# A transformer block with kernelized attention and routed experts on one core: the fifth weighing of the values moved to VectorE, the second norm's scalings put between copies, shorter GpSimd chains, a direct last store

## What is computed

```python
mod = (silu(c) @ wmod)                 # six vectors of 256 per batch row: sa, ca, ga, sb, cb, gb
h = layernorm(x) * (1 + ca) + sa       # x: 8 x 1024 x 256
x = x + ga * attention(h)
h = layernorm(x) * (1 + cb) + sb
x = x + gb * ffn(h)

# attention, 16 heads of 16: q, k, v from one product; xq, xk = clip(q / 4), clip(k / 4)
Tq, Tk = chebyshev(xq), chebyshev(xk)            # polynomials of the orders 0 to 10, 5 of which have a weight
num = sum over orders of Tq * beta * cumsum over tokens of (Tk * v)
den = sum over orders of sum(Tq) * beta * cumsum over tokens of sum(Tk)
attention = (num / (den + 1e-7)) @ W_out.T

# ffn: one shared expert and the best 2 of 8 routed ones, weights sqrt(softplus(logits)), hidden size 128
```

## Time and profile before

| | us |
|---|---|
| median of three timed runs | 977.48 |
| lowest and highest of them | 973.81, 977.93 |
| the profiled execution | 972.85 |
| its span, first to last instruction | 971.1 |
| TensorE busy | 861.6 (89%) |
| VectorE busy | 836.6 (86%) |
| GpSimd busy | 474.3 (49%) |
| ScalarE busy | 441.0 (45%) |

### The profile page before, as it was taken

How to read it: one execution, slowest core, us unless ns; L and a number is a source line. 1 busy time by engine, 2 the same in 40 slices (tenths; PEclk the granted TensorE clock), 3 DMA queues, 4 the chain that set the end, 5 groups by cost and what they waited for, 6 DMA issues and landing times. The chain is left out here.

```text
span 971.1 us, 14288 instructions
## 1 busy us (share of the span) xinstructions
PE 861.6 (89%) x4377; PEld 642.1 (66%) x4377; DVE 836.6 (86%) x1317; ACT 441.0 (45%) x636; POOL 474.3 (49%) x636
## 2 busy tenths in 40 slices
PE   5765839899999989899999999898999999979995
PEld 4535436686767676776767676766767676747784
DVE  2797879999999999999999999999999999987421
ACT  4624345554636354555535363555545363521420
POOL 2525354554637265645737274645746274443210
PEclk9786769999999999999999999999999999989998
DMA  8023125353534445364535344453534343444331
GB/s 303 1 50 88 23 67 163 67 153 74 152 81 100 126 77 159 66 155 85 163 66 141 76 91 139 82 158 67 163 69 128 76 116 98 80 124 83 121 109 22
DMA packets 52237, 101.03 MB, mean 104 GB/s; under 512 B 5380, under 2 KB 34639, under 8 KB 50135
## 3 DMA queue, kind: packets, MB, share of 16 engines
q1 hardware_dynamic: 36340, 66.14, 20.9%
q0 software_dynamic: 15360, 33.56, 20.2%
q10 hardware_dynamic: 482, 0.74, 0.2%
HBM read 57.68 MB, written 17.58 MB: 77 GB/s over the span
## 5 line engine op out<-in xcount | busy, mean ns | idle before, releaser
L1425 PE MATMUL acc<-w,hid 128*128 128x256 f32 x1152 | 272.9, 382 | 13.2 <-DVE hid L1116 13.2
L1425 PEld LDWEIGHTS acc<-w,hid 128*128 128x128 f32 x1152 | 215.7, 190 | 57.1 <-DVE hid L1116 24.1
L795 ACT ACTIVATE hid<-ring,b1row 128x512 f32<-128x512 f32 x144 | 98.5, 684 | 180.3 <-PE ring L1306 179.0
L618 POOL DMA_DIRECT2D feat<-feat x48 | 46.5, 968 | 269.4 <-DVE feat L993 132.4
L1116 DVE TENSOR_TENSOR hid<-hid,cfw 128x512 f32<-128x512 f32 x128 | 92.4, 724 | 39.0 <-DMA cfw<-cf_rows 23.6
L750 ACT ACTIVATE feat<-ring,bqkv 128x512 f32<-128x512 f32 x96 | 66.1, 689 | 112.4 <-PE ring L1306 112.4
L1306 PE MATMUL ring<-n2H,w1H 128*128 128x512 f32 x288 | 102.3, 436 | 0.0
L1383 PE MATMUL tr<-wo_g,feat 128*128 128x256 f32 x256 | 64.7, 410 | 40.0 <-DVE feat L1035 40.0
L968 DVE TENSOR_TENSOR_SCAN feat<-zero,carry,feat 128x512 f32<-128x512 f32 x80 | 99.3, 1291 | 0.0
L968 DVE TENSOR_TENSOR_SCAN feat<-zero,feat 128x512 f32<-128x512 f32 x80 | 95.8, 1247 | 0.0
L1306 PE MATMUL ring<-n2H,w1L 128*128 128x512 f32 x288 | 90.8, 396 | 0.0
(11 more groups left out here) (160 smaller groups left out, 1571.4 us busy)
## 6 DMA issues: line engine op xcount, KB each, us to landing
feat<-feat POOLq DMA_DIRECT2D x48, 512.0 KB, 4.6
cfw<-cf_rows SPq DMA_DIRECT2D x16, 1280.0 KB, 7.6
xin<-in_L_attn_x SPq DMA_DIRECT2D x16, 512.0 KB, 9.3
feat<-inv_rows SPq DMA_DIRECT2D x32, 256.0 KB
out<-x SPq DMA_DIRECT2D x16, 512.0 KB, 8.5
cfw<-cf_rows SPq DMA_DIRECT2D x16, 512.0 KB, 3.7
out<-fin POOLq DMA_DIRECT2D x16, 512.0 KB, 6.0
cfw<-cf_rows SPq DMA_DIRECT2D x16, 256.0 KB, 4.6
```

Source lines behind the costliest of these rows:

```text
L618: g.dma_start(f(into), f(of), accum_op=ALU.add).then_inc(added[n], 16)
L795: a.activation(hid[:, e % NG], ring[bank][:, :], ACT.Silu, bias=b1row[:, e:e + 1]).then_inc(ring_copied, 1)
L1425: last = mm(acc[t // 2][:, t % 2], hid[:, e % NG, t * P:(t + 1) * P], w2[:, e], start=False, stop=(e == E), skip_group_check=True)
```

## The change

Five edits.

1. The weighing of order 4 (`KT5 * V0`) leaves GpSimd (`weigh_order_5` and its semaphore go) and becomes the fourth of five weighings on VectorE, after expert 3 and ahead of the weighing of order 2 (order `BY_WEIGHT`). The waits on the counts follow.
2. `normalise_second` is called four times, one scaling behind each of the four k and q copies. The first call has the two waits, the last one raises the semaphore.
3. `inv_std` (both norms) has ten operations for twelve: the halving of the mean is folded into the variance's constants, and the inverse deviation is doubled at the end.
4. For the last chunk alone: no store of x1, and no accumulating store. `last_output` on VectorE gates each bank, adds x1, and SyncE stores each half of the output directly. SyncE's last waits follow.
5. For the last chunk alone: TensorE holds back the `expert_down` of experts 6 and 7 and does those of 6, 7 and 8 for bank 0 first, then for bank 1 (`last_experts_by_bank`).

```diff
@@ inv_std
-            nc.gpsimd.tensor_tensor(t(0), m0, m1, ALU.add).then_inc(mv_steps[n], 1)
             nc.gpsimd.tensor_tensor(t(1), m0, m1, ALU.subtract).then_inc(mv_steps[n], 1)
             nc.gpsimd.tensor_tensor(t(2), s0, s1, ALU.add).then_inc(mv_steps[n], 1)
-            pool.wait_ge(mv_steps[n], NMV * c + 3)
-            nc.gpsimd.tensor_tensor(t(3), t(0), k_("half", NT), ALU.mult).then_inc(mv_steps[n], 1)
-            nc.gpsimd.tensor_tensor(t(4), t(1), k_("half", NT), ALU.mult).then_inc(mv_steps[n], 1)
-            nc.gpsimd.tensor_tensor(t(5), t(2), k_("1/D", NT), ALU.mult).then_inc(mv_steps[n], 1)
+            nc.gpsimd.tensor_tensor(t(0), m0, m1, ALU.add).then_inc(mv_steps[n], 1)
+            pool.wait_ge(mv_steps[n], NMV * c + 2)
+            nc.gpsimd.tensor_tensor(t(6), t(1), t(1), ALU.mult).then_inc(mv_steps[n], 1)
+            nc.gpsimd.tensor_scalar(t(7), t(2), 4.0 / D, 4.0 * EPS_LN, ALU.mult, ALU.add).then_inc(mv_steps[n], 1)
+            pool.wait_ge(mv_steps[n], NMV * c + 5)
+            nc.gpsimd.tensor_tensor(t(8), t(6), t(7), ALU.add).then_inc(mv_steps[n], 1)
+            nc.gpsimd.tensor_scalar(t(10), t(0), -1.0, None, ALU.mult).then_inc(mv_steps[n], 1)
             pool.wait_ge(mv_steps[n], NMV * c + 6)
-            nc.gpsimd.tensor_tensor(t(6), t(4), t(4), ALU.mult).then_inc(mv_steps[n], 1)
-            nc.gpsimd.tensor_tensor(t(7), t(5), k_("eps", NT), ALU.add).then_inc(mv_steps[n], 1)
+            nc.gpsimd.tensor_tensor(t(3), t(8), k_("-half", NT), ALU.pow).then_inc(mv_steps[n], 1)
             pool.wait_ge(mv_steps[n], NMV * c + 8)
-            nc.gpsimd.tensor_tensor(t(8), t(6), t(7), ALU.add).then_inc(mv_steps[n], 1)
-            pool.wait_ge(mv_steps[n], NMV * c + 9)
-            nc.gpsimd.tensor_tensor(t(9), t(8), k_("-half", NT), ALU.pow) \
-                .then_inc(mv_steps[n], 1)
-            nc.gpsimd.tensor_tensor(t(10), t(0), k_("-half", NT), ALU.mult).then_inc(mv_steps[n], 1)
-            pool.wait_ge(mv_steps[n], NMV * c + 11)
-            nc.gpsimd.tensor_tensor(t(11), t(10), t(9), ALU.mult).then_inc(rstd_ready[n], 1)
+            nc.gpsimd.tensor_tensor(t(9), t(3), t(3), ALU.add).then_inc(mv_steps[n], 1)
+            nc.gpsimd.tensor_tensor(t(11), t(10), t(3), ALU.mult).then_inc(rstd_ready[n], 1)
@@ SyncE
-                if loads or i < B:
+                if i < B and not is_last(i, p):
                     store_x1(i, p)
...
+            for h in range(2):
+                sp.wait_ge(out_added, h + 1)
+                sp.dma_start(o_v[B - 1, CB - 1][:, 2 * h:2 * h + 2], fin[:, 2 * h:2 * h + 2]).then_inc(last_stored, 16)
...
+            sp.wait_ge(last_stored, 2 * 16)
@@ GpSimd
-                g.tensor_tensor(f(W + 4), f(KT5), f(V0), ALU.mult).then_inc(weighted5, 1)
...
-                    weigh_order_5(i, p)
...
-                if st["ffn"]:
+                if st["ffn"] and not is_last(*later(i, p, -2)):
                     add_to_output(*later(i, p, -2))
@@ ScalarE
-                for half in HALVES[:4]:
+                for t, half in enumerate(HALVES[:4]):
                     copy(half)
-                if second:
-                    normalise_second(act, *prev)
+                    if second:
+                        normalise_second(act, *prev, t)
@@ VectorE
-            BY_WEIGHT = (0, 1, 3, 2)
+            BY_WEIGHT = (0, 1, 3, 4, 2)
...
+                    dve.wait_ge(odd_ready, 4 * c + n // 2)
+                    v.tensor_tensor(f(W + n), f(KT3 if n == 2 else KT5), val, ALU.mult).then_inc(weighted, 1)
...
+            def last_output(i, p):
+
+                dve.wait_ge(gate_loaded[1], 16 * (i + 1))
+                dve.wait_ge(stored[1 - p], 16 * (i + p))
+                for h in range(2):
+                    rows = fin[:, 2 * h:2 * h + 2]
+                    dve.wait_ge(bank_done, h + 1)
+                    v.tensor_tensor(rows, acc[h][:, :, :], gate(1), ALU.mult).then_inc(ffn_gated, 1)
+                    dve.wait_ge(ffn_gated, 2 * number(i, p) + h + 1)
+                    v.tensor_tensor(rows, rows, x1[:, p, 2 * h:2 * h + 2], ALU.add).then_inc(out_added, 1)
...
                 expert(3)
                 if attn_:
                     weigh(i, p, 3)
+                    weigh(i, p, 4)
                     prefix(i, p, 2)
                     prefix(i, p, 3)
@@ TensorE
+            def last_experts_by_bank(i, p):
+
+                c = number(i, p)
+                for h in range(2):
+                    for e in (E - 2, E - 1, E):
+                        if h == 0:
+                            pe.wait_ge(hidw_ready, E * c + e)
+                        for t in (2 * h, 2 * h + 1):
+                            last = mm(acc[h][:, t % 2], hid[:, e % NG, t * P:(t + 1) * P], w2[:, e], start=False,
+                                      stop=(e == E), skip_group_check=True)
+                    last.then_inc(bank_done, 1)
```

More of the change, by code:

```diff
@@ L234, in build @@
         weighted = sem("values_weighted")
-        weighted5 = sem("values_weighted_order_5")
         scanned = sem("prefix_sums")
@@ L257, in build @@
         hidw_ready = sem("hidden_weighted")
-        expert_done = sem("expert_done")
+        expert_done, bank_done = sem("expert_done"), sem("bank_done")
+        out_added, last_stored = sem("output_added"), sem("last_stored")
         ffn_gated = sem("ffn_gated")
-        NLOG, NSOFT, NCF, NSPLIT, NMV = 7, 10, 3, 7, 11
+        NLOG, NSOFT, NCF, NSPLIT, NMV = 7, 10, 3, 7, 9
         late_products, late_biases, late_weights = (sem(f"late_{n}") for n in ("bias_products", "biases", "weights"))
@@ L286, in number, with is_last @@
             return CB * i + p
+        def is_last(i, p):
+            return isinstance(i, int) and number(i, p) == CB * B - 1
         def later(i, p, n):
@@ L386, in normalise_first, with normalise_second @@
             last.then_inc(norm_ready[0], 1)
-        def normalise_second(act, i, p):
+        def normalise_second(act, i, p, t):
             c = number(i, p)
[L391 to L396, removed]
+            if t == 0:
+                act.wait_ge(rstd_ready[1], c + 1)
+                ge(act, transposed[1], 2 * c)
+            last = nc.scalar.activation(ntok[:, t], x1[:, p, t], ACT.Identity, bias=ms[:, 1, 11, t:t + 1],
+                                        scale=ms[:, 1, 9, t:t + 1])
+            if t == NT - 1:
+                last.then_inc(norm_ready[1], 1)
         def load(sp, i, p):
@@ L591, in _ @@
                     step(i, p, True, False)
-            for p in range(CB):
-                sp.wait_ge(x1_stored[p], 16 * B)
-                sp.wait_ge(stored[p], 16 * B)
+            for h in range(2):
+                sp.wait_ge(out_added, h + 1)
+                sp.dma_start(o_v[B - 1, CB - 1][:, 2 * h:2 * h + 2], fin[:, 2 * h:2 * h + 2]).then_inc(last_stored, 16)
+            sp.wait_ge(x1_stored[0], 16 * B)
+            sp.wait_ge(stored[0], 16 * B)
+            sp.wait_ge(x1_stored[CB - 1], 16 * (B - 1))
+            sp.wait_ge(stored[CB - 1], 16 * (B - 1))
+            sp.wait_ge(last_stored, 2 * 16)
         @block.gpsimd
@@ L599, in _ @@
             g = nc.gpsimd
-            def weigh_order_5(i, p):
-                c = number(i, p)
-                pool.wait_ge(odd_ready, 4 * c + 2)
-                ge(pool, numerator, c)
-                g.tensor_tensor(f(W + 4), f(KT5), f(V0), ALU.mult).then_inc(weighted5, 1)
             def add_orders(i, p, n):
@@ L747, in copy_qkv @@
                 if m >= 4:
-                    ge(act, weighted, (ND - 1) * number(i, p))
-                    ge(act, weighted5, number(i, p))
+                    ge(act, weighted, ND * number(i, p))
                 a.activation(feat[:, (K0 + p, Q0 + p, V0)[m // 2], m % 2], ring[bank][:, :], ACT.Identity,
@@ L762, in square @@
                     if q == 0:
-                        ge(act, weighted, (ND - 1) * c)
-                        ge(act, weighted5, c)
+                        ge(act, weighted, ND * c)
                     else:
@@ L953, in weigh @@
                 else:
-                    dve.wait_ge(odd_ready, 4 * c + 1)
-                    v.tensor_tensor(f(W + n), f(KT3), val, ALU.mult).then_inc(weighted, 1)
+                    dve.wait_ge(odd_ready, 4 * c + n // 2)
+                    v.tensor_tensor(f(W + n), f(KT3 if n == 2 else KT5), val, ALU.mult).then_inc(weighted, 1)
             def prefix(i, p, j):
@@ L960, in prefix @@
                 n = ORDERS[j]
-                if n < 4:
-                    dve.wait_ge(weighted, (ND - 1) * c + BY_WEIGHT.index(n) + 1)
-                else:
-                    dve.wait_ge(weighted5, c + 1)
+                dve.wait_ge(weighted, ND * c + BY_WEIGHT.index(n) + 1)
                 if p:
@@ L1200, in step @@
                 if ffn:
-                    output(*exp)
+                    (last_output if is_last(*exp) else output)(*exp)
                 if qkv:
@@ L1437, in expert @@
                             expert_up(*exp, use, e + 2)
```

(5 more changed lines are left out.)

## The result

| | before | after |
|---|---|---|
| median of four runs | 977.70 | 988.11 |
| lowest and highest | 973.81, 979.94 | 985.47, 990.69 |
| the profiled execution | 972.85 | 990.69 |
| its span | 971.1 | 989.0 |

The ratio is 1.0124, with an interval of 1.0087 to 1.0162: slower by 10.4 us between the medians. The two profiled executions differ by 17.8, because that of before was faster than all four timed ones and that of after the slowest of its four.

What follows compares the result with a forecast made beforehand. TensorE bounds each step's first half (21.9 us), VectorE the second (31.4). Terms -0.3 -0.3 +14.8 -0.9 -0.9 +1 +0.3 -3.4 sum to +10.3: 983.2 on the profiled execution, 987.8 on the median; predicted 986.5, range 975 to 1000.

Steps and rivals of the forecast that it cites:

- What bounds the kernel: Each step: TensorE sets the first 21.9 us, VectorE the next 31.4; VectorE work counts only from the second norm's low halves.
- The weighing, +14.8: VectorE's added multiplication after expert 3's last weighted tile: 1.14 us in each of chunks 2 to 14, +14.8.
- second halves: Part of each step from VectorE's start on the second norm's low halves to TensorE's next projection; 31.4 us at VectorE's pace.
- The freed stalls, nothing: About 29 us of VectorE rows lengthened under GpSimd's multiplication, in the half TensorE sets; counted at nothing, with exceptions.
- Chunks 0 and 1, -0.3 each: Chunk 0: 1.14 less 1.48 of freed stall; chunk 1: 1.14 less 1.5 of shorter wait for the second norm's scalings.
- Chunk 2's gates, -0.9: GpSimd's scaling of output weights by the gates should come earlier, off VectorE's second half: -0.9 (0 to -2).
- Chunks 10 and 12, -0.9: Rest of TensorE's waits for the second norm's scalings, saved by placing the scalings between the copies: -0.9.
- The late steps, +1: Six steps where GpSimd's chain ends after the first copy's start, so the first scaling delays later copies: +1 (0 to +6).
- the two signs that I had named for being wrong: A full step's period not growing by about 1.1 us, or ScalarE's copies being spread apart.
- the second rival: ScalarE blocked: chains end as late as today in late steps, TensorE loses about 19 us, 1001 to 1006; chance 0.13.
- Chunk 15, +0.3: Last chunk, chain on the path: 1.14 for the weighing less 0.8 for two fewer chain operations, +0.3.
- The end, -3.4: Last output by direct half-size stores from SyncE, landing at 964.8 instead of 968.2: -3.4 (-4.1 to -0.8).

## Why the forecast of the total held, and which terms did not

Predicted 986.5, measured 988.11. The change was forecast as +10.3; it is +10.4 between the medians and +12.1 by the ratio. By the terms:

- **What bounds the kernel** held. Weighings before the low halves are nearly free once GpSimd's is gone, and behind them they cost about 1.14 us each: shown in both directions, by the kernel with the multiplication left out (30.7 us less work, 5.3 gained) and by those with one and both moved early (17.5 and 32.9 gained).
- **The weighing, +14.8.** The two traces give +11.7 in the second halves of chunks 2 to 14 (0.90 each, not 1.14) and +3.1 in chunks 1 and 15. The kernel with this edit alone is +15.3 (11.2 to 19.2) by its ratio. In that kernel's trace chunks 2 to 14 have +15.1. The size per chunk scatters from +0.2 to +2.34 in two single traces. Chunk 14, where TensorE waited 2.8 us for the division, is not the weighing's doing, at least not wholly: its second half is 2.1 to 2.2 longer than in before with the chains alone and with the last output alone too. In after, VectorE waits 1.97 there for the transfer of the inverse, for 0.71 in before; why is open.
- **The freed stalls, nothing.** Nearly right: they became idle time, but leaving the multiplication out alone is worth 5.3 (2.7 to 7.8), of which I had counted 2.4, in chunks 0 and 2.
- **Chunks 0 and 1, -0.3 each.** What stands before chunk 1's ring is -0.7 once the 3.9 of the start-up is taken off. In chunk 1 the wait for the scalings fell from 2.73 to 1.26, the 1.5 that I counted, but its first half stayed (+0.1), and the second grew by 1.7. The chunk is +1.8, not -0.3. Of the 1.5, 1.1 is lost ahead of the copies: the first one starts 16.16 after the projection for 15.07, at a granted clock of 0.75 on the mean of the half for 0.78. The kernels with the weighing or the chains alone have that too (16.51 and 16.22).
- **Chunk 2's gates, -0.9.** The collision is gone: GpSimd's scaling starts at 164.97, 1.0 ahead of the low halves, and VectorE's row behind them (timeline of after) takes 1.22 where it took 2.14:

```profile
167.32 1.22 DVE L985 SCALAR_TENSOR_TENSOR feat<-feat 128x1024 f32<-128x1024 f32 x1
```

The sum does not show it: the chunk is +0.9, where 1.14 - 0.9 was expected; what took its place is open.

- **Chunks 10 and 12, -0.9.** The gain is there, though not by edit 2: their first halves stood 0.45 and 0.94 above 21.87 in before, and with the short chains alone they are 21.89. In after it is buried under the next term, which falls on the same chunks (23.34 in both).
- **The late steps, +1.** The mis-sized term. I had two cases, the power slips in ahead of VectorE's multiplication (nothing) or it doesn't (up to 1.0 too late), and took the first. It missed in all six steps, by 0.01 us in chunk 10 (595.72 against 595.71). In five of them the chain's last operation was held as well, and in chunk 6, where it was not, nothing was lost. TensorE waits 5 x 1.2 = 6.0 in the list; the first halves of chunks 4, 8, 10, 12 and 14 stand 1.2 to 1.5 above 21.87, 7.1 together; and moving the scalings back saves some 5 us by the ratios. That is the upper bound, +6, not +1. It is also one of the two signs that I had named for being wrong, ScalarE's copies spread apart (3.16 for 1.40), and the condition of the second rival, met in five steps at 1.2 us each. An order of two instructions that rests on 0.2 us is no order to count on. Nor was my list of late steps (3, 6, 8, 10, 12, 14) the one that came out (4, 6, 8, 10, 12, 14).
- **Chunk 15, +0.3.** It is +2.2. TensorE's longest wait for the scalings, there, is 4.4 in place of 4.6, so the shorter chain gave some 0.2, not 0.8; 1.4 of the rest is in the second half.
- **The end, -3.4.** It is -7.1 in the traces and -8.3 (-12.1 to -4.6) by the ratio of its own kernel: outside my bounds (-4.1 to -0.8) in the good direction. Two things were mis-sized. The store landed 2.1 after its issue, and I had taken 3.7, from rows of twice the size. And I had left out GpSimd's drain: before, the span went on for 2.9 us after the accumulating store had landed (968.2 to 971.1); behind the direct one 0.5 is left. The Trainium skill (DMA: Bandwidth & Descriptors, Anatomy of one DMA) makes the landing an estimated 2.6, by a formula that it states for transfers issued by GpSimd; this one is SyncE's, and the measured 2.1 is below the estimate, nearer to it than to my 3.7.

So the total is right in part by luck: two errors cancel, since the late steps cost some 5 more than I took, and the end gave 4 to 5 more. The second rival happens when the chains stay long, and costs more than its 19 us: with the scalings alone the kernel is 25.8 slower. That it then takes 1006.09, at the top of the rival's 1001 to 1006, says nothing, for it lacks the added weighing.

## What to carry to other kernels

Find the place in a step where the bounding engine changes, and cost an instruction by the side of it on which it stands: the same multiplication was worth about 1.14 us behind that place and next to nothing ahead of it, so moving it gained more than any of the five edits. Do not put a wait for another engine's chain between copies that free the matrix engine's banks, unless the chain ends earlier by a margin that the profile shows. Edits that touch the same chain are to be timed together: here +25.8 and +1.1 became +5 (12.1 - 15.3 + 8.3). And ask which engine closes the program: a transfer that GpSimd issues last is followed by its drain.

## What the runs showed of the hardware

- After a wait of 4.3 us TensorE came back at the lower clock for part of the next 12 us (0.72 on the mean), which added 2.7 us to the wait; after a wait of 1.2 us in chunk 10 of after, its first pair took 0.73 and the next ones 0.62 to 0.64 as before.
- GpSimd operations on 128x4, whose like took 0.20 to 1.1 us, were held for 3.16, 3.29 and 4.64 us under rows of VectorE operations that followed each other without a gap. One of them, with the same start beside VectorE's rows, took 0.70 in one chunk and 1.83 in five: whether it gets in between is not settled by the order of the starts to 0.01 us.
- Two direct stores of 256 KB landed 2.1 us after their issue, where the accumulating stores of 512 KB take 6.2 (the list of DMAs of after), and the end of the program came 0.5 after the direct one in place of 2.9.
- GpSimd's closing drain ended 2.7 us after the landing of its last transfer, in before (968.2 to 970.9) and in after (967.6 to 970.3).
